# Path attention of a two-layer Perceiver block: the block inverse kept as 32x32 diagonal tiles

## The chip, the cores and the metric

The kernel runs on one core of a Trainium2 chip. The metric is the device time of one execution in microseconds (us), lower is better. The core has five engines that work at the same time: TensorE (PE, matrix multiplies; PEld is its weight load), VectorE (DVE), ScalarE (ACT), GpSimd (POOL) and SyncE (SP, which issues DMAs). They meet through semaphores. SBUF is the on-chip memory, 128 partitions wide; PSUM is where TensorE writes, 8 banks of 512 float32 values in each partition.

## The reference, cut to what matters

Input x is (16, 64, 256): 16 batch rows of 64 tokens. Six stages follow each other: cross attention, linear attention, a top-2 mixture of experts, a filtered cross attention with feed-forward, path attention, an expert-choice mixture. Only path attention changes. There are 16 heads of 16 channels, and each has two directions, so 32 systems of 64x64 for each batch row:

```python
wh = Wdir ...                       # unit vectors, (b, 32, 64, 16)
Mw  = jnp.where(strict, einsum('bhtd,bhsd->bhts', wh, wh) * bh[..., None], 0.0)
rhs = jnp.where(strict, einsum('bhtd,bhjd->bhtj', wh, kh) * bh[..., None], 0.0)
Bmat = solve_triangular(Mw + eye(t), rhs, lower=True)
# logits = q k^T - (lower part, with diagonal, of q w^T) @ Bmat
# then a causal softmax, the mean over the values, and the output projection
```

All of it is float32.

## The kernel before, in words

`path_attention` (L1688) is stage 5. It has two parts. The first (L1718 to L1943) makes the layer norm, the projections q, k, w, w times beta (`wb`) and v, and on POOL the constant masks. The second part, the batch loop (from L1996 on), is written out for the 16 batch rows without a hardware loop. Its instructions are in program order on each engine; nothing but semaphores and this order decides who works when.

The 32 systems of a batch row lie as 4 groups g by 4 heads j by 2 directions; the two directions of a pair sit in the lower and the upper 64 partitions. `mq` holds the masked transposed system and q times w, `mr` the masked right-hand side and the first inverse. The batch loop does, for batch row b:

- ACT copies the four operands of the row into one tile, `moving` (L2166). POOL spreads w and wb over pairs (`spread`, L1994) into `wt`, `wbt`, which are the weights of the products below.
- PE `strips` (L2041): two sets of 16 products with 32 rows, 128 weight columns and 128 moving columns. DVE masks them (L2251, L2254) and adds the identity (L2256); POOL makes the level masks `cT` (L2006, L2017) and the first transposed inverse (L2009, L2011), group by group.
- PE `logits` (L2067, then `small`) of the row before; DVE adds the causal mask (L2226), takes the maximum (L2232) and subtracts it (L2234); ACT takes the exponential (L2171).
- Block inverse: `inv` and `invT` are 64x64 for each system. Four levels n (block sizes 2, 4, 8, 16) of: PE `small(cT, inv)` into x, ACT copies x out (L2189), PE `small(invT, x)` and `small(x, invT)`, DVE subtracts from both inverses (L2265, L2267). In between stand the turned probabilities (L2077), the product with v (L2087) and the turned output (L2094) of the row before.
- The fifth level (block size 32) is not built into the inverse: three `small` products y = invT rhs, z = cT y, w = invT z, copied by ACT (L2206, L2209), and DVE's sol = y - w (L2274).

`small` (L2047) is the product that all of this uses. It covers one group g with 8 products of 64 rows, 64 weight columns and 64 moving columns, two at a time on the two halves of the partitions:

```python
def small(at, g, column, left, right, **flags):
    for j in range(4):
        for rows in half:
            mm = mmul(ps[rows, at, column + j * T:column + (j + 1) * T], left[rows, g, j, :],
                      right[rows, g, j, :], **flags)
    return mm
```

In float32 the trace shows two MATMUL records and two LDWEIGHTS records for each such product (transposes have one of each); counts below are of records.

Of the kernel before, what the change touches and what calls it, by code (L numbers as in the profile page):

```python
# [1687 lines left out]
def path_attention(core):  # L1688
# [10 lines left out]
    LEVELS = (2, 4, 8, 16, 32)  # L1699
    with ExitStack() as stack:  # L1700
# [6 lines left out]
        mq_mask, mr_mask = sb("upper_and_minus_incl", [P, 2, T]), sb("minus_first_and_below", [P, 2, T])  # L1707
        same, levelT = sb("same_block", [P, T]), sb("levelT", [P, len(LEVELS), T])
        firstT, causal = sb("minus_firstT", [P, T]), sb("causal", [P, T])
        ident_c = sb("ident_compact", [P, T])  # L1710
# [4 lines left out]
        with ExitStack() as inner:  # L1715
# [29 lines left out]
            def _(pool):  # L1745
# [6 lines left out]
                upper, mincl, below_first, below = mq_mask[:, 0], mq_mask[:, 1], mr_mask[:, 0], mr_mask[:, 1]  # L1752
                for o, value in ((upper, 1.0), (mincl, -1.0), (below, 1.0), (causal[:], 0.0), (below_first, 1.0),
                                 (ident_c[:], 0.0), (blocks[:], 1.0)):
                    c.link(g.memset(o, value))
                halves = (slice(0, T), slice(T, P))
                for rows in halves:
                    select(mq_mask[rows, 0], [[1, T]], -1, -1, 0.0)
                    select(mq_mask[rows, 1], [[1, T]], 0, -1, 0.0)
                    select(mr_mask[rows, 0], [[-1, T]], -1, 1, 0.0)  # L1760
                    select(mr_mask[rows, 1], [[-1, T]], -1, 1, 0.0)
                    select(causal[rows, :], [[-1, T]], 0, 1, -1e30)
                    select(ident_c[rows, :], [[-1, T]], 0, 1, 1.0, ALU.not_equal)

                def same_blocks(s, o):

                    c.link(g.memset(o[:], 1.0))
                    for rows in halves:
                        select(o[rows], [[-s, T // s], [0, s]], 0, 1, 0.0)
                        select(o[rows], [[s, T // s], [0, s]], s - 1, -1, 0.0)  # L1770

                same_blocks(2, same)
                c.link(g.tensor_tensor(firstT[:], same[:], upper, ALU.mult))
                c.link(g.tensor_scalar(firstT[:], firstT[:], -1.0, None, ALU.mult))
                c.link(g.tensor_tensor(below_first, same[:], below_first, ALU.mult))
                c.link(g.tensor_scalar(below_first, below_first, -1.0, None, ALU.mult))
                for n, s in enumerate(LEVELS):
# [4 lines left out]
                    c.link(g.tensor_tensor(m, m, upper, ALU.mult))  # L1782
# [164 lines left out]
        mq, mr = sb("mt_and_qw", [P, G, 4, 2, T]), sb("m_and_rhs", [P, G, 4, 2, T])  # L1947
        cT = sb("cT", [P, 2, G, 4, T])
        both_inv, x = sb("inv_and_invT", [P, G, 2, 4, T]), sb("x", [P, G, 4, T])
        inv, invT = both_inv[:, :, 0], both_inv[:, :, 1]  # L1950
        moving = sb("moving", [P, 2, G, 2, T])

        wt, wbt, qt = (sb(n, [P, G, 2, T]) for n in ("wt", "wbt", "qt"))
        kt = sb("kt", [P, G, T])
        vt = sb("vt", [P, 8, 2, 16])
        sol = sb("sol", [P, G, 4, T])
        y, z = sb("y", [P, G, 4, T]), sb("z", [P, G, 4, T])
        qwn = sb("qwn", [P, G, 4, T])
# [6 lines left out]
        moving_ready, spread_ready, qk_ready, vt_ready = (sem(n) for n in  # L1965
            ("moving_ready", "w_spread", "qk_ready", "vt_ready"))
        mq_ps, mq_sb, mr_ps, mr_sb, qwn_sb = (sem(n) for n in
            ("mt_qw_in_psum", "mt_qw_ready", "m_rhs_in_psum", "m_rhs_ready", "qwn_ready"))
        inv_step, start_sb, level_ready = sem("inv_step"), sem("start_ready"), sem("level_ready")
# [11 lines left out]
        with ExitStack() as inner:  # L1981
# [8 lines left out]
            def _(pool):  # L1990
# [6 lines left out]
                def batch(b, first):  # L1997
# [4 lines left out]
                    for dst, n in ((wt, 1), (wbt, 0)):  # L2002
                        spread(dst, moving[:, n, :, 0, :]).then_inc(spread_ready, 1)
# [601 lines left out]
```

## Time and profile before

| | us |
|---|---|
| median of 3 runs | 3066.19 (3065.31 to 3066.53) |
| the profiled execution | 3066.14 |
| its span, first to last instruction | 3064.4 |
| the batch loop of path attention inside it | 660, from 2160 to 2820 |
| one batch row inside the loop | 41.1 |
| busy of the whole span: PE, DVE, ACT, POOL | 2611.6, 1781.3, 1084.1, 753.5 |

The profile is of one execution. A row of it gives an engine, a line of the kernel, the operation, the tiles, the shape (for a product: rows*weight columns, then rows x moving columns) and a count; x64 is 64 records. "[idle before <-releaser]" is the time that the engine stood before the first record of the row, and what ended it; `issue` means that nothing in the profile ended it. PEclk is the share of TensorE's full clock that was granted.

### The profile page before, as it was taken

To read this page: it belongs to the slowest core of one execution; us is meant where nothing else is said; L and a number is where in the kernel's file an instruction comes from. 1 tells how busy PE (TensorE), PEld (TensorE's weight loads), DVE (VectorE), ACT (ScalarE), POOL (GpSimd) and SP (SyncE) were. 2 spreads that over 40 slices of the span, in tenths; PEclk is the share of its full clock that TensorE was granted. 3 is DMA by queue.
4 is the path that set the end of the run, shared out by engine and by line. 5 is a ranking of instruction groups with operands and counts; after the bars stand their busy time and mean duration, and the time that the engine had idled before them with its cause. 6 is when DMAs were issued, how large, how long until landed. Compare 5 with 4: busy or idle time off the path is not lost. (4 is left out here: it accounts for less than half of the span.)

```text
span 3064.4 us, 78538 instructions
## 1 busy us (share of the span) xinstructions
PE 2611.6 (85%) x34608; PEld 1894.5 (62%) x34608; DVE 1781.3 (58%) x2561; ACT 1084.1 (35%) x1702; POOL 753.5 (25%) x964
## 2 busy tenths in 40 slices
PE   5998988988897979988888878777688999888598
PEld 3565555555555545545555554443688898888487
DVE  4655545545454444569999975537666556665500
ACT  2443433434343211145555542216233333332121
POOL 6900000000000000012333323030565556663200
PEclk9999999989898779989999988889899998999699
DMA  2101001001000001132322201000000000000131
GB/s 63 33 18 34 18 18 34 18 18 32 20 2 22 0 26 36 50 94 66 93 71 82 82 17 48 0 20 14 3 4 3 4 4 4 4 3 3 55 137 41
DMA packets 24535, 99.16 MB, mean 32 GB/s; under 512 B 4824, under 2 KB 9837, under 8 KB 19502
## 3 DMA queue, kind: packets, MB, share of 16 engines
q1 hardware_dynamic: 24238, 94.57, 10.6%
q8 instruction: 264, 4.33, 0.6%
q14 instruction: 33, 0.27, 0.0%
HBM read 93.51 MB, written 1.05 MB: 31 GB/s over the span
## 5 line engine op out<-in xcount | busy, mean ns | idle before, releaser
L611 DVE TENSOR_REDUCE xa_minus_max_parts<-psum 128x4 f32<-128x1600 f32 (+1 forms) x128 | 233.9, 1827 | 221.9 <-PE psum L331 221.9
L628 DVE TENSOR_TENSOR xa_probT<-psum,xa_minus_max_spread 128x2048 f32<-128x2048 f32 (+1 forms) x112 | 239.6, 2139 | 200.5 <-PE psum L350 200.5
L315 PE MATMUL psum<-xa_ctxT,xa_wk 96*128 96x400 f32 (+1 forms) x512 | 217.7, 551 | 0.9 <-issue 0.8
L536 ACT ACTIVATE xa_probT<-xa_probT,zero_column 128x2048 f32<-128x2048 f32 (+1 forms) x112 | 209.4, 1870 | 10.8 <-DVE xa_probT L628 10.8
L2017 POOL TENSOR_TENSOR pa_cT<-pa_mt_and_qw,pa_levelT 128x256 f32<-128x256 f32 x256 | 192.6, 787 | 69.4 <-PE psum L2051 69.4
L322 PE MATMUL psum<-xa_wv,xa_ctxT 96*128 96x256 f32 (+1 forms) x832 | 208.0, 392 | 0.0
L1279 POOL TENSOR_TENSOR tk_exp_all<-tk_exp_all,tk_exp_left 128x577 f32<-128x577 f32 x64 | 120.9, 1890 | 354.2 <-ACT tk_exp_left L1400 354.2
L2189 ACT ACTIVATE pa_x<-psum 128x256 f32<-128x256 f32 x256 | 98.4, 384 | 306.3 <-PE psum L2051 294.1
L2265 DVE TENSOR_TENSOR pa_inv_and_invT<-pa_inv_and_invT,psum 128x512 f32<-128x512 f32 x192 | 132.0, 688 | 126.9 <-PE psum L2051 126.9
L716 POOL MEMSET la_v<- 128x512 f32 x1 | 0.5, 525 | 809.2 <-remote 809.2
L2051 PE MATMUL psum<-pa_inv_and_invT,pa_cT 64*64 64x64 f32 x4096 | 153.6, 237 | 40.3 <-DVE pa_prob L2226 36.7
L350 PE MATMUL psum<-xa_qb,xa_kT 32*128 32x128 f32 (+1 forms) x3328 | 132.7, 297 | 61.9 <-issue 29.4
L350 PEld LDWEIGHTS psum<-xa_qb,xa_kT 32*128 32x128 f32 (+1 forms) x3328 | 112.0, 195 | 115.4 <-issue 109.3
L322 PEld LDWEIGHTS psum<-xa_wv,xa_ctxT 96*128 96x128 f32 (+1 forms) x832 | 145.7, 185 | 60.7 <-ACT xa_v L528 27.5
L1447 DVE MAX8 tk_top<-tk_left 128x8 f32<-128x1601 f32 x96 | 175.1, 1824 | 4.1
L2051 PEld LDWEIGHTS psum<-pa_inv_and_invT,pa_cT 64*64 64x64 f32 x4096 | 144.5, 152 | 48.3 <-issue 44.4
L1449 DVE MATCH_REPLACE8 tk_left<-tk_top,tk_left 128x1601 f32<-128x1601 f32 x96 | 173.9, 1811 | 0.0
L1352 PE MATMUL psum<-tk_ctx,tk_attnT 128*128 128x192 f32 (+1 forms) x832 | 147.5, 336 | 14.7 <-ACT tk_attnT L1406 14.0
L1332 PE MATMUL psum<-tk_ctxT,tk_qwt 97*128 97x512 f32 (+1 forms) x256 | 128.2, 585 | 36.8 <-ACT tk_ctxT L1422 32.6
L2051 PE MATMUL psum<-pa_inv_and_invT,pa_x 64*64 64x64 f32 x4096 | 158.6, 220 | 0.0
L1352 PEld LDWEIGHTS psum<-tk_ctx,tk_attnT 128*128 128x128 f32 (+1 forms) x832 | 138.8, 195 | 21.3 <-ACT tk_attnT L1406 21.3
L528 ACT ACTIVATE xa_v<-psum 128x512 f32<-128x512 f32 (+1 forms) x112 | 63.5, 567 | 233.1 <-PE psum L322 233.1
(471 smaller groups left out, 5143.0 us busy)
## 6 DMA issues: line engine op xcount, KB each, us to landing
tk_ctx<-in_ctx SPq DMA_DIRECT2D x16, 1248.0 KB, 5.5
xa_ctxT<-in_ctxT SPq DMA_DIRECT2D x16, 1200.8 KB, 7.4
tk_ctxT<-in_ctxT SPq DMA_DIRECT2D x16, 1200.8 KB
ec_w<-in_ec_w SPq DMA_DIRECT2D x16, 1024.0 KB, 6.8
m_gate_up<-in_m_gate_up SPq DMA_DIRECT2D x17, 256.0 KB, 2.6
m_down<-in_m_down SPq DMA_DIRECT2D x17, 128.0 KB, 2.5
ff_w<-in_ff_w SPq DMA_DIRECT2D x2, 1024.0 KB
x_resident<-in_x SPq DMA_DIRECT2D x1, 1024.0 KB, 4.8
```

The source lines that it names most:

```text
L315: mm = mmul(ps[:, KEY_BANK[n], 0:z - a], wk[:, k, m * P:(m + 1) * P], ctxT[:, h, k, a:z], start=(k == 0), stop=(k == 1))
L322: mm = mmul(ps[0:width(c), VALUE_BANK[g], (c % 2) * D:(c % 2 + 1) * D], ctxT[:, h, k, c * P:c * P + width(c)], wv[:, k, :], start=(k == 0) ...
L350: mm = mmul(ps[0:w, j, (2 * r + c) * P:(2 * r + c + 1) * P], kT[quad[j], h, r, at:at + w], qb[quad[j], h, r, :, :].rearrange("p e t -> p ( ...
L536: a_(o, o, ACT.Exp, bias=core.zero[0:w]).then_inc(e_done, 1)
L611: v_.tensor_reduce(part[:, :, n % 2, n // 2], ps[:, 0:4, 0:z - a], AX.X, ALU.max, negate=True).then_inc(m_used, 1)
L628: v_.tensor_tensor(o[:, :, 0:chunks], got[:, :, 0:chunks], shift[0:w].unsqueeze(2).broadcast_to([w, 8, chunks, P]), ALU.add).then_inc(sub_ ...
L1352: mm = nc.tensor.matmul(flat[:, CCOL:CCOL + C], aT[0:width(c), c, :], ctx[0:width(c), h, c, :], start=(c == KC - 1), stop=(c == 7))
L1447: c.step(nc.vector.max(best, src))
L1449: c.step(nc.vector.match_replace(left[:, u % 2, :], best, src, TAKEN))
L2017: g_.tensor_tensor(cT[:, n % 2, g], mq[:, g, :, 0, :], four(levelT[:, n, :]), ALU.mult).then_inc(level_ready, 1)
L2051: mm = mmul(ps[rows, at, column + j * T:column + (j + 1) * T], left[rows, g, j, :], right[rows, g, j, :], **flags)
L2265: v.tensor_tensor(whole, whole, ps[:, 4 + g, :], ALU.subtract).then_inc(inv_sb, 1)
```

## The change

The inverse is kept only as its two 32x32 diagonal tiles for each system, so `mt`, `cT`, `inv`, `invT` and `x` have 32 columns where they had 64. `blocks32` takes the place of `small` in the four levels: one group g is 16 products of 32x32 with 32 moving columns, four at a time on the diagonal of the array. The solve is written out: the upper half of the solution (rows 0 and 2 of the four 32-row strips), a product with the corner tile of the system, a subtraction from the right-hand side, the lower half. `moving`, `kt`, `qwn`, `z` and their copies are gone; products read `wb`, `q`, `k` in place. The system of the next row is made by 96 small products (`mt_strips`) during the solve, and copied out by ACT. POOL's masks become one instruction for all four groups; the subtraction of the maximum goes from DVE to POOL; DVE makes the first inverse by 32x32 transposes. Tiles that cross a row boundary have two buffers.

The core of the diff, first PE's:

```diff
-                def small(at, g, column, left, right, **flags):
+                def blocks32(bank, column, left, right, rows=(0, 1, 2, 3), shift=0, n=Q):
                     for j in range(4):
-                        for rows in half:
-                            mm = mmul(ps[rows, at, column + j * T:column + (j + 1) * T], left[rows, g, j, :],
-                                      right[rows, g, j, :], **flags)
+                        for r in rows:
+                            mm = mmul(ps[quad[r + shift], bank, column + j * n:column + (j + 1) * n], left[quad[r], j, :],
+                                      right[quad[r], j, 0:n], start=True, stop=True)
                     return mm
+                def mt_strips(b):
+                    pe.wait_ge(wt_ready, b + 1)
+                    if b >= 2:
+                        pe.wait_ge(ot_sb, KD * (b - 1))
+                    if b:
+                        pe.wait_ge(x_sb, G * NI * b)
+                    for j in range(4):
+                        for h in range(2):
+                            for kk, column, cols in ((0, 2 * P, 0), (1, 2 * P, 1), (0, 3 * P, 1)):
+                                for g in range(G):
+                                    mm = mmul(ps[quad[2 * h + kk], g, column + j * Q:column + (j + 1) * Q],
+                                              wt[quad[g], j, h, kk * Q:(kk + 1) * Q],
+                                              wb[quad[g], j, b * T + cols * Q:b * T + (cols + 1) * Q], start=True, stop=True)
+                                    if j == 3 and h == 1 and column == 3 * P:
+                                        mm.then_inc(mt_ps, 1)
+                def qw_strips(b):
+                    pe.wait_ge(mt_sb, G * b + G)
+                    strips(0, wt, q[:, :, at(b)], qw_ps)
+                def batch(b):
+                    inv, invT = inv_of(b), invT_of(b)
+                    if b:
+                        logits_from_keys(b - 1)
+                        pe.wait_ge(sol_sb, G * b)
+                    pe.wait_ge(wbt_ready, b + 1)
+                    strips(4, wbt, k[:, :, at(b)], rhs_ps)
+                    if b:
+                        logits_from_solution(b - 1)
                     for n in range(NI):
+                        pe.wait_ge(level_ready, NI * b + n + 1)
                         for g in range(G):
...
+                            blocks32(g, 0, cT[:, n % 2, g], inv[:, g]).then_inc(x_ps, 1)
                         for g in range(G):
...
                             if n < NI - 1:
-                                small(4 + g, g, 0, invT, x, start=True, stop=True)
-                            small(4 + g, g, 4 * T, x, invT, start=True, stop=True).then_inc(t_ps, 1)
+                                blocks32(4 + g, 0, invT[:, g], x[:, g])
+                            blocks32(4 + g, P, x[:, g], invT[:, g]).then_inc(t_ps, 1)
+                        if b and n:
+                            (turn_probs, weigh, turn_out)[n - 1](b - 1)
                     for g in range(G):
+                        pe.wait_ge(inv_sb, G * (NI * b + NI - 1) + g + 1)
+                        blocks32(4 + g, 0, invT[:, g], rhs[:, g], rows=(0, 2), n=T).then_inc(y_ps_, 1)
+                    if b + 1 < B:
+                        mt_strips(b + 1)
                     for g in range(G):
+                        pe.wait_ge(y_sb, G * b + g + 1)
+                        blocks32(4 + g, 2 * P, mt[:, b % 2, g, 1], y[:, g], rows=(0, 2), shift=1).then_inc(z_ps, 1)
+                    if b + 1 < B:
+                        qw_strips(b + 1)
                     for g in range(G):
+                        pe.wait_ge(z_used, G * b + g + 1)
+                        blocks32(4 + g, 0, invT[:, g], rhs[:, g], rows=(1, 3), n=T).then_inc(sol_ps, 1)
```

POOL's, ACT's and DVE's batch, new side only:

```diff
+                def batch(b):                                   # POOL
+                    pool.wait_ge(mt_sb, G * b + G)
...
+                    level(b, 0)
+                    g_.tensor_tensor(invT_of(b), diagonal(b), over_g(firstT[:]), ALU.mult).then_inc(first_step, 1)
+                    pool.wait_ge(first_step, b + 1)
+                    g_.tensor_tensor(invT_of(b), invT_of(b), over_g(ident_c[:]), ALU.add).then_inc(firstT_ready, 1)
...
+                    level(b, 1)
+                    if b:
+                        shift(b - 1)
+                        pool.wait_ge(log_ps, G * b)
+                    spread(qt, q[:, :, at(b)]).then_inc(qt_ready, 1)
...
+                def copy_mt(b):                                 # ACT, after the four copies of y
+                    for g in range(G):
+                        act.wait_ge(mt_ps, G * b + g + 1)
+                        a.activation(mt[:, b % 2, g].rearrange("p a j c -> p (a j c)"), ps[:, g, 2 * P:4 * P], ACT.Copy
+                                     ).then_inc(mt_sb, 1)
...
+                def batch(b):                                   # DVE
                     for g in range(G):
+                        rhs_out(b, g)
+                        if b:
+                            log_out(b - 1, g)
+                    if b:
+                        maxima(b - 1)
                     for n in range(NI):
...
+                    for g in range(G):
+                        dve.wait_ge(z_ps, G * b + g + 1)
+                        v.tensor_tensor(rhs[:, g, :, 0:Q], rhs[:, g, :, 0:Q],
+                                        ps[:, 4 + g, 2 * P:3 * P].rearrange("p (j c) -> p j c", j=4),
+                                        ALU.subtract).then_inc(z_used, 1)
+                    if b + 1 < B:
+                        qw_out(b + 1)
+                        first_inverse(b + 1)
```

The mask constants on POOL are made in 32-row strips, four where there were two halves, 32 columns wide where they were 64, and for four levels where there were five.

## Rows read from the trace of the kernel before

**Rows 1.** Windows of the batch loop, a row of it, a slow stretch (us, busy and count by engine, PEclk, DMA):

```profile
2160.00:2820.00 660.00, 592.83 (x17286) 576.68 (x17286) 396.35 (x650) 220.47 (x536) 396.93 (x528) 0.94 0.01 4
2365.00:2406.00 41.00, 36.74 (x1082) 35.76 (x1082) 24.86 (x42) 13.92 (x34) 24.69 (x34) 0.96 0.02 4
2208.40:2211.80 3.40, 3.40 (x71) 3.40 (x68) 2.34 (x2) 2.31 (x6) 3.40 (x4) 0.50 0.02 5
```

**Rows 2.** Timeline of PE over one batch row (start us, us, then the group):

```profile
2407.63 1.12 PE L2067 MATMUL psum<-pa_kt,pa_qt 32*128 32x64 f32 x32 [1.76 <-DVE pa_mt_and_qw L2251]
2408.68 2.08 PE L2051 MATMUL psum<-pa_sol,pa_qwn 64*64 64x64 f32 x64
2413.46 3.48 PE L2051 MATMUL psum<-pa_inv_and_invT,pa_cT 64*64 64x64 f32 x64 [2.70 <-DVE pa_prob L2226]
...
2427.38 1.97 PE L2087 MATMUL psum<-pa_vt,pa_probT 128*128 128x32 f32 x16
...
2441.04 2.03 PE L2051 MATMUL psum<-pa_y,pa_cT 64*64 64x64 f32 x64
2442.91 2.03 PE L2051 MATMUL psum<-pa_z,pa_inv_and_invT 64*64 64x64 f32 x64
2444.87 1.17 PE L2041 MATMUL psum<-pa_moving,pa_wt 32*128 32x128 f32 x32
2445.86 1.07 PE L2041 MATMUL psum<-pa_moving,pa_wbt 32*128 32x128 f32 x32
2448.69 1.12 PE L2067 MATMUL psum<-pa_kt,pa_qt 32*128 32x64 f32 x32 [1.75 <-DVE pa_mt_and_qw L2251]
```

**Rows 3.** Timeline of PE in the first stage, products of 17 weight columns:

```profile
308.68 1.09 PE L361 MATMUL psum<-xa_probT,xa_v 128*17 128x64 f32 x64
309.70 1.61 PE L315 MATMUL psum<-xa_ctxT,xa_wk 96*128 96x400 f32 x4
```

**Rows 4.** DMA queues from 2160 to 2820 (packets, MB, share of 16 engines):

```profile
q8 instruction: 137, 2.24, 1.4%
```

**Rows 5.** DMA from 2187 to 2197, 40 slices of 0.25 us; q8 alone moved data:

```profile
GB/s 0 0 66 0 0 0 0 0 0 0 0 0 0 0 0 0 0 66 0 0 0 0 0 0 0 0 0 0 0 0 0 0 0 66 0 0 0 0 0 0
```

**Rows 6.** Timeline of the weight loads, inside that stretch and at 2733:

```profile
2193.59 0.20 PEld L2051 LDWEIGHTS psum<-pa_y,pa_cT 64*64 64x64 f32 x4
2193.99 1.77 PEld L2051 LDWEIGHTS psum<-pa_y,pa_cT 64*64 64x64 f32 x58 [0.21 <-issue]
...
2733.05 0.54 PEld L2051 LDWEIGHTS psum<-pa_z,pa_inv_and_invT 64*64 64x64 f32 x16 [0.18 <-issue]
```

**Rows 7.** DMA from 2729 to 2735, 40 slices of 0.15 us:

```profile
GB/s 0 0 0 0 0 0 0 109 0 0 0 0 0 0 0 0 0 0 0 0 0 0 0 0 0 0 0 0 0 0 0 0 0 0 109 0 0 0 0 0
```

**Rows 8.** Timeline of PE after a hardware loop jumped back; DMA from 293.5, slices of 0.125 us:

```profile
296.58 2.09 PE L350 MATMUL psum<-xa_qb,xa_kT 32*128 32x128 f32 x32 [6.07 <-issue]
...
GB/s 0 0 234 0 0 0 0 0 0 0 0 0 0 0 0 0 0 0 0 0 0 0 0 0 0 0 0 0 0 131 0 0 0 0 0 0 0 0 0 0
q8 instruction: 2, 0.03, 3.0%
```

**Rows 9.** Groups of POOL, DVE and ACT (line, shapes, count | busy us, mean ns | idle):

```profile
L1140 POOL TENSOR_TENSOR powers_t<-powers_wr,filter_zr 128x512 f32<-128x512 f32 x2 | 2.5, 1267 | 0.2
L2341 POOL TENSOR_TENSOR ec_hot<-ec_hot,ec_p 128x1024 f32<-128x1024 f32 x8 | 19.8, 2513 | 39.2 <-PE psum L2369 39.2
L2265 DVE TENSOR_TENSOR pa_inv_and_invT<-pa_inv_and_invT,psum 128x512 f32<-128x512 f32 x192 | 132.0, 688 | 126.9 <-PE psum L2051 126.9
L2267 DVE TENSOR_TENSOR pa_inv_and_invT<-pa_inv_and_invT,psum 128x256 f32<-128x256 f32 x64 | 27.0, 422 | 36.4 <-PE psum L2051 34.3
L2234 DVE TENSOR_TENSOR pa_prob<-pa_prob,pa_mx 128x1024 f32<-128x1024 f32 x16 | 19.6, 1226 | 0.5
L2189 ACT ACTIVATE pa_x<-psum 128x256 f32<-128x256 f32 x256 | 98.4, 384 | 306.3 <-PE psum L2051 294.1
L2181 ACT ACTIVATE pa_q<-psum 128x128 f32<-128x128 f32 x32 | 7.1, 275 | 60.6 <-PE psum L2094 60.6
```

More of the change, by code:

```diff
@@ L1751, in _ @@
                 c.step(g.memset(eps[:], 1e-6))
[L1752 to L1761, printed above, removed]
+                for o, value in ((upper, 1.0), (mincl, -1.0), (below, 1.0), (causal, 0.0), (ident_c, 0.0), (blocks, 1.0)):
+                    c.link(g.memset(o[:], value))
@@ L1762, in _ @@
+                for rows in (slice(0, T), slice(T, P)):
+                    select(mincl[rows, :], [[1, T]], 0, -1, 0.0)
+                    select(below[rows, :], [[-1, T]], -1, 1, 0.0)
                     select(causal[rows, :], [[-1, T]], 0, 1, -1e30)
-                    select(ident_c[rows, :], [[-1, T]], 0, 1, 1.0, ALU.not_equal)
+                quads = [slice(Q * n, Q * n + Q) for n in range(4)]
+                for rows in quads:
+                    select(upper[rows, :], [[1, Q]], -1, -1, 0.0)
+                    select(ident_c[rows, :], [[-1, Q]], 0, 1, 1.0, ALU.not_equal)
@@ L1781, in _ @@
                     c.link(g.tensor_tensor(same[:], m, same[:], ALU.add))
-                    c.link(g.tensor_tensor(m, m, upper, ALU.mult))
+                    c.link(g.tensor_tensor(m, m, upper[:], ALU.mult))
                 select(blocks[:], [[-16, P // 16], [0, 16]], 0, 1, 0.0)
@@ L2035, in _, with strips @@
                 mmul = nc.tensor.matmul
-                def strips(at, left, right, done):
+                def strips(first_bank, left, right, done, **flags):
                     for j in range(4):
                         for g in range(G):
-                            mm = mmul(ps[:, at + g, j * P:(j + 1) * P],
-                                      left[quad[g], j, :, :].rearrange("p a t -> p (a t)"),
-                                      moving[quad[g], right, j, :, :].rearrange("p a t -> p (a t)"), start=True, stop=True)
-                            if j == 3:
+                            mm = mmul(ps[:, first_bank + g, j * T:(j + 1) * T],
+                                      left[quad[g], j, :, :].rearrange("p a t -> p (a t)"), right[quad[g], j, :],
+                                      start=flags.get("start", True), stop=flags.get("stop", True),
+                                      skip_group_check=not flags.get("stop", True))
+                            if j == 3 and done is not None:
@@ L2123, in batch @@
-                            small(g, g, 0, cT[:, n % 2], inv, start=True, stop=True).then_inc(x_ps, 1)
+                                pe.wait_ge(first_ready, b + 1)
+                                pe.wait_ge(*((log_sb, G * (b - 1) + g + 1) if b else (qw_sb, g + 1)))
+                            else:
+                                pe.wait_ge(inv_sb, G * (NI * b + n - 1) + g + 1)
+                            if b and g == 2 and n == 2:
+                                pe.wait_ge(pt_sb, 2 * b)
@@ L2141, in batch @@
+                    if b + 1 < B:
+                        qw_strips(b + 1)
                     for g in range(G):
-                        ready((z_sb, G * b + g + 1))
-                        small(4 + g, g, 0, invT, z, start=True, stop=True).then_inc(w_ps, 1)
+                        pe.wait_ge(z_used, G * b + g + 1)
+                        blocks32(4 + g, 0, invT[:, g], rhs[:, g], rows=(1, 3), n=T).then_inc(sol_ps, 1)
+                mt_strips(0)
+                qw_strips(0)
                 for b in range(B):
-                    batch(b, b == 0)
@@ L2147, in _ @@
-                logits(B - 1, last=True)
+                    batch(b)
+                logits_from_keys(B - 1, last=True)
+                logits_from_solution(B - 1)
                 turn_probs(B - 1)
```

278 lines of the change are left out of this document (123 added, 155 removed).

## The prediction

> **What bounds the kernel now.** I read the windows first: the batch loop takes 660 us of the span, and in one row of 41 us PE is busy 36.7, DVE 24.9, POOL 24.7 and ACT 13.9 [rows 1]. So PE sets the pace there. The timeline of PE shows how: a row begins every 41.06 us (2407.63 to 2448.69), and PE stands only twice, 1.76 us until DVE has masked the system and 2.70 us until DVE has masked the logits [rows 2]. Everything else is PE issuing products. After the second stand it works for 3.4 us at a granted clock of 0.50, its lower level (1.2 GHz) [rows 1], and 64 records take 3.30 us there instead of 1.87.
>
> How fast does PE issue? In the solve 64 records start in 1.87 us (2441.04 to 2442.91), 29.2 ns each [rows 2]. Each has a weight load beside it (17286 and 17286 in the loop [rows 1]), so an instruction leaves every 14.6 ns. The reader is to see a second limit close behind this one. The DMA queue q8 carries PE's instructions: 137 packets of 16 KB for 34572 records, 252 per packet [rows 4, 1], in 1.4% of 16 engines over 660 us, 1.1 us a packet. Where PE runs at full speed the packets start 3.75 and 4.0 us apart [rows 5], which is the 3.7 us that 252 records last. And PE runs dry: at 2193.99 and 2733.05 weight loads stand with nothing in the profile to release them [rows 6]. The packet before the first began in the slice at 2191.25 to 2191.5, the one before the second at 2730.05 to 2730.2 [rows 5, 7]: the stand ends 2.6 and 2.9 us after the packet's start, its length of 1.1 and some 1.5 us more, both times, and the next packet starts 1.1 to 1.4 us later, 4.05 us after the one before in [rows 7]. So one block is fetched ahead, not many. The jump of a hardware loop shows the same: packets 3.4 us apart (27 slices of 0.125), PE's first product (296.58) 2.8 us after the first packet and 0.55 before the second [rows 8]. The loop lives just under its instruction supply.
>
> **The change part by part.**
>
> Instructions of PE, one batch row, in MATMUL records. Before: 1082 [rows 1]. After, from the diff (records are twice the products, once for transposes): levels, four times 128 for x, three times 256 and once 128 for the update, 1408, where they were 704; y, z and the lower solve 64 each, as the three products before; system of the next row 192; q w and right-hand side 32 each, where two sets of 32 were; logits 32 and 64; the turned and weighed parts 26 as before. Sum 1978, 83% more, and as many weight loads: 3956 instructions, or 15.7 blocks of 252 where there were 8.6.
>
> Array time of these. A 32x32 product was not run before. From the nearest rows: halving the moving columns and going from two to four at once makes 29.2 into 7.3 ns a record; the products of 17 weight columns and 64 moving columns, four at once, start every 15.9 ns (64 in 1.02 us [rows 3]), and they are of the size that is twice as long. From above, a record could cost what it costs now, 29.2. I take 7.3 for the array. Levels and system: 1600 x 7.3 = 11.7 us; z, two at once, 64 x 14.6 = 0.9; y, lower solve and logits 3 x 1.87; the two strip sets 2 x 0.99; keys 1.05; weighing 16 x 119 ns = 1.9; ten transposes at the same 119, 1.2 [rows 2]. That is 24.4 us, so the array would no longer be the bound.
>
> Supply. 15.7 blocks a row at the interval of a starved fetch. The rows give 3.4 (jump), 3.75 and 4.0 us [rows 5, 8]. When PE empties a block faster, the request for the next should come earlier in it, so I take the shortest, 3.4; 4.0 is the upper end. Whole loop: 16 x 3956 = 63296 instructions, 251 blocks, 251 x 3.4 = 853 us. Nearly each block is shorter than that for the array: the one with the 16 weighings is 1.9 + 0.8 us, half a block of y with half of the system 1.9 + 0.5. So the array hides behind the supply, not the other way round.
>
> Clock. In the levels PE would then stand more than half of the time. In the rows its clock fell to half after stands that long [rows 1, 2]. For the 32x32 products this costs nothing, since they still fit under 3.4 us. For y, the lower solve, logits, strips and weighing it doubles 11.7 us, of which the supply hides part. Between 0 and 10 us a row; I take 2, since the slow stretch of [rows 1] was over after 3.4 us in which PE worked: 32 us.
>
> Waits. The stands of 1.76 and 2.70 us go as such (the system is made in the row before; logits and right-hand side are masked in turns). New ones: `qw_strips` waits for ACT's four copies of `mt`; 256 wide they take 0.38 each [rows 9], 1.6 us with the latency, against z's 128 instructions. Behind the copy stands POOL: level mask, first inverse and identity, 3 x 1.27 for 512 columns [rows 9], 3.8 us; then DVE's four transposes (128 wide, not in the trace; ACT's 0.28 to DVE's 0.42, 1.2 us), and behind them in DVE's order the eight maskings, 3.2. That is 8.2 us from the copy to the last mask, while PE has the 448 instructions of q w, lower solve, keys, right-hand side and logits, 6.0 us of supply, and the first three groups of level 0, 1.3. Left: 0.9 us. I count 0.8 a row, 13 us; bounds 0 and 3 us, what the two stands cost now.
>
> The subtraction of the maximum on POOL costs 2.5 instead of 1.23 us [rows 9]. Between it and the turned probabilities PE has two levels, six blocks, so it is hidden in rows 1 to 15 and adds 1.3 us after the last. ACT's x copies halve (0.38 to 0.28) and DVE's updates shrink from 0.69 to 0.42 [rows 9]; both wait for PE. The four copies of `moving`, POOL's copy of k and ACT's of q w run beside PE today and bring nothing now. The mask constants: some 16 more short selects on POOL, beside the projections; if that cover failed, under 5 us. Tile buffers change no time.
>
> Sum. Loop: 853 + 32 + 13 = 898 us, plus 1 at the end, against 660: +239. On the profiled execution (3066.14, practically the median of 3066.19): 3305 us. A batch row would take 56 us.
>
> The Trainium skill speaks against this. "Runtime: NRT & Kernel Launch", section "Instruction fetch mechanics", says that instructions come in 16 KiB blocks, that PE holds eight, and that crossing a boundary is mostly hidden since a dispatch floor of about 20 cycles per instruction is slower. The stands at 2193.99 and 2733.05 show that it is not hidden at 14.6 ns an instruction, and 14.6 ns held for hundreds is under 20 cycles of the 1.2 GHz sequencer (16.7 ns, an estimate from that page and "TensorE: Matmul & The Clock Gate"). With that floor instead of the supply a row would be 66 us.
>
> **The rivals.**
>
> A, the supply keeps up (a deeper prefetch once blocks are emptied fast). Then the array and the waits count: 24.4 us a row, plus 0.7 for the `mt` copy, 1.6 for the masks before level 0 and about 1.3 around probabilities and output, 28 us; 660 - 16 x 13.1 + 1 = 451, and 2857 us. For it: 64 products with their loads left in 1.02 us [rows 3], 8 ns an instruction. Against it: 128 instructions are half a block, and the fastest stretch of the loop, the solve, gives 3.7 us to 252 [rows 2]. The skill's page on the runtime, with fetches hidden, is this rival without its dispatch floor. This is the other side. It turns on the block interval: under 2.6 us (41.1 / 15.7) the kernel gets faster.
>
> B, blocks overlap in part, so that the 1.5 us after a packet is not paid each time: 1.1 + 1.1 = 2.2 us, 34.5 a row, with waits and heavy blocks 37: -66, 3001 us. For it: the packets are short. Against it: both stands and the jump came with 1.5 us or more.
>
> C, a record costs the same whatever its size: 29.2 ns. Levels, system and z 1664 x 29.2 = 48.6, the rest 11.7, a row of 60.3: +307, 3373 us. Against it the 15.9 ns of [rows 3]. "TensorE: Matmul & The Clock Gate" of the Trainium skill, "Back-to-back issue gap", gives a floor of about 25 ns between matmuls however small. By it a row is an estimated 53.3 us and the kernel near 3262; the 15.9 ns disagrees.
>
> D, the change doesn't cut the array time because the diagonal tiles don't run at once: 1600 records at 14.6 ns, 23.4 + 12.7 = 36 us, under the supply, so the time is mine.
>
> **How the numbers follow.** Forecast with D 0.78, C 0.05, A 0.10, B 0.07. Bounds of the forecast: blocks at 3.25 with no clock loss and no wait, 816 us, +157: 3223; blocks at 4.0 with 2 us of clock and 0.8 of waits, 1004 + 46, +390: 3456. The range is 3160 to 3450: it leaves out A, B and a twentieth of the forecast. Two runs of this kernel are told apart from 0.2% (6 us). Slower: D, C and nearly no other, 0.82; faster A and most of B, 0.16; same 0.02, where B's interval comes to 2.6 us.
>
> **What would show it.** Right: some 250 packets on q8 in the loop at 3.3 to 3.6 us without a gap; PE's share of busy in the levels well under one half, stands before PE and its weight loads ended by `issue`; a row of 52 to 60 us; the granted clock in the loop clearly under 0.94; no engine over 60% busy. Wrong: packets closer than 2.6 us; rows of 128 level records that start in about 1 us one behind the other (A), or in 3.7 us evenly (C); stands in the levels that end at DVE or ACT.

## The result

The changed kernel takes 3414.7 us (median of 4 runs, 3407.6 to 3417.9) where the kernel before takes 3065.8 (4 runs, 3060.9 to 3066.5): a ratio of 1.114, with an interval of 1.112 to 1.115. It is 349 us slower; the prediction said 3305 us, 239 slower, with a range up to 3450. The profiled execution has a span of 3410.5 us, 346 more than before, and its batch rows account for that: counted from the first key product of one row to that of the next, the mean of ten rows is 62.96 us instead of 41.28, and 16 x 21.7 is 347. The number lies in the range but 110 us over the forecast, so what speaks for the mechanism is not the number: rival C, at 3373 us, came nearer to it. The traces and the runs below decide.

### The profile page after: what moved, and what is told of

It is laid out like the page before. It is cut to its first block and busy times, and to the rows that moved or that the text cites. A ratio compares the mean times of both kernels' runs of the same rounds, so it can differ in the third digit from the quotient of the medians.

```text
span 3410.5 us, 106580 instructions
## 1 busy us (share of the span) xinstructions
PE 2740.5 (80%) x48944; PEld 1996.3 (59%) x48944; DVE 1633.9 (48%) x2545; ACT 1035.7 (30%) x1686; POOL 562.8 (17%) x623
## 5 line engine op out<-in xcount | busy, mean ns | idle before, releaser
L2302 DVE TENSOR_TENSOR pa_inv_and_invT<-pa_inv_and_invT,psum 128x256 f32<-128x256 f32 x192 | 80.9, 421 | 381.7 <-PE psum L2065 380.4
L2065 PE MATMUL psum<-pa_x,pa_inv_and_invT 32*32 32x32 f32 x6144 | 135.5, 222 | 150.1 <-issue 150.1
L2228 ACT ACTIVATE pa_x<-psum 128x128 f32<-128x128 f32 x256 | 70.9, 277 | 486.2 <-PE psum L2065 466.9
L2065 PE MATMUL psum<-pa_inv_and_invT,pa_x 32*32 32x32 f32 x8192 | 160.1, 227 | 56.2 <-issue 56.2
L2065 PEld LDWEIGHTS psum<-pa_x,pa_inv_and_invT 32*32 32x32 f32 x6144 | 108.9, 135 | 163.8 <-issue 163.7
L2065 PEld LDWEIGHTS psum<-pa_inv_and_invT,pa_x 32*32 32x32 f32 x8192 | 137.1, 141 | 54.9 <-issue 54.9
L2065 PE MATMUL psum<-pa_inv_and_invT,pa_cT 32*32 32x32 f32 x8192 | 123.1, 227 | 36.7 <-issue 36.5
L2065 PEld LDWEIGHTS psum<-pa_inv_and_invT,pa_cT 32*32 32x32 f32 x8192 | 112.3, 141 | 47.7 <-issue 44.6
```

Of the source, the lines that this page charges most:

```text
L2065: mm = mmul(ps[quad[r + shift], bank, column + j * n:column + (j + 1) * n], left[quad[r], j, :], right[quad[r], j, 0:n], start=True, stop= ...
```

## The profile after

The page's lines first: busy time of PE, the granted clock in 40 slices of the span, and the queue that carries PE's instructions.

```profile
PE 2740.5 (80%) x48944; PEld 1996.3 (59%) x48944; DVE 1633.9 (48%) x2545; ACT 1035.7 (30%) x1686; POOL 562.8 (17%) x623
...
PEclk9999999899986998999997889555556565565699
...
q8 instruction: 375, 6.14, 0.8%
```

The windows answer to [rows 1]: the same 660 us of the loop, one row, and the part of it with q w, lower solve, keys, right-hand side and logits.

```profile
2160.00:2820.00 660.00, 468.36 (x20751) 439.94 (x20755) 163.62 (x419) 113.81 (x342) 140.23 (x119) 0.57 0.02 4
2410.50:2474.60 64.10, 44.40 (x1980) 41.58 (x1979) 15.71 (x40) 10.96 (x33) 12.98 (x11) 0.61 0.02 4
2405.00:2417.70 12.70, 12.70 (x228) 12.17 (x224) 5.15 (x17) 1.53 (x4) 2.80 (x3) 0.50 0.01 3
```

A row has 1980 records (1978 were counted). DVE, ACT and POOL are busy for 15.7, 11.0 and 13.0 us of its 64.1, where the row before had 24.9, 13.9 and 24.7 of 41. PE is idle for 20 us of the row, and over the loop its clock is at 0.57 instead of 0.94. The waits of PE say who owns the 20 us; this is the view of waits over fifteen rows, from 2220 to 3160 (line that waited, what ended the wait, us in total, times, longest), all of its lines:

```profile
PE psum L2065 <- issue: 237.5, 133, 2.7
PE psum L2080 <- issue: 20.0, 15, 2.5
PE psum L2125 <- issue: 1.7, 2, 1.3
PE psum L2115 <- issue: 1.4, 1, 1.4
PE psum L2054 <- issue: 0.7, 1, 0.7
```

Not one of them ends at DVE, ACT or POOL. The two stands of before, at DVE [rows 2], are gone as the change meant; PE now waits for its own instructions. The timeline of PE over a row answers to [rows 2]:

```profile
2403.20 1.91 PE L2065 MATMUL psum<-pa_y,pa_mt_and_corner 32*32 32x32 f32 x62 [1.64 <-issue]
2405.04 1.98 PE L2054 MATMUL psum<-pa_q,pa_wt 32*128 32x64 f32 x32
2406.95 3.62 PE L2065 MATMUL psum<-pa_rhs,pa_inv_and_invT 32*32 32x64 f32 x64
2410.51 1.98 PE L2098 MATMUL psum<-pa_k,pa_qt 32*128 32x64 f32 x32
2412.27 1.93 PE L2054 MATMUL psum<-pa_k,pa_wbt 32*128 32x64 f32 x32
2414.13 3.68 PE L2107 MATMUL psum<-pa_sol,pa_minus_qw 64*64 64x64 f32 x64
2417.74 1.42 PE L2065 MATMUL psum<-pa_inv_and_invT,pa_cT 32*32 32x32 f32 x128
...
2422.46 0.21 PE L2065 MATMUL psum<-pa_x,pa_inv_and_invT 32*32 32x32 f32 x1 [2.40 <-issue]
...
2426.14 0.26 PE L2065 MATMUL psum<-pa_x,pa_inv_and_invT 32*32 32x32 f32 x2 [2.32 <-issue]
...
2430.12 0.69 PE L2065 MATMUL psum<-pa_inv_and_invT,pa_cT 32*32 32x32 f32 x35 [2.06 <-issue]
```

The 128 records of the first level start in 1.27 us (2417.74 to 2419.01), 9.9 ns each: the small products do run beside each other. Then comes the pattern of the levels: a little over a microsecond of work, then a stand of 1.6 to 2.5, every 3.5 to 4.0 us. Over the first two levels PE is busy for half of the time:

```profile
2417.70:2438.00 20.30, 10.15 (x770) 9.44 (x768) 4.65 (x10) 3.25 (x9) 7.39 (x6) 0.67 0.02 4
```

The queue has the same beat. From 2419 to 2427, in slices of 0.2 us, it moved two packets (compare [rows 5, 7]):

```profile
GB/s 0 0 0 82 0 0 0 0 0 0 0 0 0 0 0 0 0 0 0 0 0 0 0 82 0 0 0 0 0 0 0 0 0 0 0 0 0 0 0 0
```

By their records these packets begin at 2419.66 and 2423.70 and last 1.34 and 1.02 us. The stands end at 2422.46 and 2426.14, which is 1.46 and 1.42 us after a packet's end, the 1.5 us of the kernel before. Of 115 distances between packets from 2230 to 2700 the shortest is 3.26 us, the median 3.78 and the mean 4.05; 85% are under 4.5, with a mean of 3.74. Over all 230 distances from 2220 to 3160 the median is 3.76, and that is the value used below. Of the 17 distances over 4.5, the longest (up to 7.6) touch the part from q w to the logits, where a window above shows a clock of 0.50 and 12.7 us; six, of 4.5 to 5.1, stand by the weighing, or by the turned output and y, at a clock of 0.50 to 0.55.

## The experiments

Kernels sent together were timed beside the kernel before on the same chip (3060.7 to 3066.5 us). The row is the mean of ten, from one profile; packets are those of q8.

| kernel | PE records a row | packets a row | us | row, us | clock in the loop |
|---|---|---|---|---|---|
| before | 1082 | 8.6 | 3065.8 | 41.3 | 0.94 |
| after | 1978 | 15.5 | 3414.7 | 63.0 | 0.58 |
| dose | 2234 | 17.6 | 3527.6 | 70.5 | 0.57 |
| cols | 1978 | 15.5 | 3407.4 | 62.4 | 0.82 |
| fill | 2010 | 15.8 | 3444.4 | 65.3 | 0.61 |
| warm | 2014 | 15.8 | 3428.6 | 63.1 | 0.90 |
| mt48 | 1882 | 14.8 | 3398.6 | 62.1 | 0.58 |
| half | 1178 | 9.3 | 3024.0 | 38.8 | 0.54 |
| wide64 | 1114 | 8.7 | 3046.4 | 39.7 | 0.92 |
| wide64b | 1114 | 8.7 | 3010.0 | 37.3 | 0.97 |
| before_dose | 1338 | 10.6 | 3135.0 | 44.9 | 0.96 |
| wide64h | 666 | 5.3 | 2855.4 | 27.6 | 0.76 |

**More instructions, hardly more work: dose.**

```diff
+                            if n in (1, 2):
+                                blocks32(g, 0, cT[:, n % 2, g], inv[:, g])
                             blocks32(g, 0, cT[:, n % 2, g], inv[:, g]).then_inc(x_ps, 1)
```

> The changed kernel with the 128 records of x at the second and third level issued twice (the same values into the same place): +256 records, +512 instructions a row, 2 blocks. Supply theory: +2 x 3.75 = 7.5 us a row, +120 us: 3535 (3510 to 3550), fetches on q8 up by 32. Rival, latency between the engines (ACT's copies, DVE's updates) fills the levels: the records cost 9.9 ns each where they have to be issued, 2.5 us a row or less, +40: 3455 or below.

3527.6 us, +113. Two more packets a row (2.1) and 7.5 us more: 3.6 us each. At the 9.9 ns a record of the changed kernel the array time of the 256 added records is an estimated 2.5 us, a third of that.

**More work, the same instructions: cols.**

```diff
-                            blocks32(g, 0, cT[:, n % 2, g], inv[:, g]).then_inc(x_ps, 1)
+                            pair = both_inv[:, b % 2, g].rearrange("p a j c -> p (a j) c")
+                            blocks32_wide(g, 0, cT[:, n % 2, g], pair, 0).then_inc(x_ps, 1)
```

(`blocks32_wide` moves 64 columns; the two updates are changed in the same way.)

> The changed kernel with every product of the four levels moving 64 columns instead of 32 (the neighbouring tile's columns with it, which nobody reads): the same 3956 instructions a row and the same values, but the array work of 1408 records a row doubled, +10.3 us at the full clock, +20.6 at half. Supply theory: 2816 instructions are 11 blocks of 3.5 us, 38.5 us, and the doubled products need 20.6 us at the full clock, 41 at half: between -8 us a row (the fuller array raises the granted clock and the other parts of the row run at full speed) and +4: 3290 to 3480. If the array set the pace: +10 to +20 us a row, 3575 to 3740. What the clock does under it is the second question: it stays at 0.58 if small products are not the reason for it.

3407.4 us, and 1.114 times the kernel before beside it, the ratio of the changed kernel. Doubling the array work of 1408 records a row cost nothing. Its timeline shows the fuller work: 28 records take 0.75 us (2426.31 to 2427.06), where the changed kernel has 29 in 0.38 (2430.63 to 2431.01), both at about half clock.

```profile
2422.07 1.45 PE L2076 MATMUL psum<-pa_inv_and_invT,pa_cT 32*32 32x64 f32 x89
2425.77 0.69 PE L2076 MATMUL psum<-pa_inv_and_invT,pa_cT 32*32 32x64 f32 x34 [2.25 <-issue]
2426.31 0.94 PE L2076 MATMUL psum<-pa_x,pa_inv_and_invT 32*32 32x64 f32 x28
2427.06 1.04 PE L2076 MATMUL psum<-pa_inv_and_invT,pa_x 32*32 32x64 f32 x28
```

The part from q w to the logits is at half clock as in the changed kernel, in its windows:

```profile
2463.10:2475.90 12.80, 12.80 (x229) 12.22 (x232) 5.19 (x16) 1.54 (x4) 3.46 (x3) 0.50 0.01 3
```

The clock over the loop rose from 0.58 to 0.82 and brought under 1 us a row, since it rose in the levels (1.00 from 2422 to 2424 in cols), where PE waits for the queue.

**Work put into the stands: fill.**

```diff
+                            mmul(ps[:, 4 + g, 3 * P:4 * P], core.ident[:], core.ident[:], start=True, stop=True)
                             if n < NI - 1:
```

> The changed kernel with 16 products a row added in the levels, one ahead of each group's update (identity by identity, 128 columns, into a part of PSUM that nobody reads): 64 instructions, a quarter of a block, but 3.4 us of array work at the full clock, 6.8 at half. Supply theory with the clock as its second part: the stands are long enough to hold this work, so +0.9 us a row (+15 us) for the instructions; and if the granted clock rises because PE stands less, the parts of the row that run at half clock now (upper and lower solve, right-hand side, logits) get shorter, up to -8 us a row: 3300 to 3430. Rival, the array is the bound in the levels: +3.4 to 6.8 us a row, 3470 to 3525.

3444.4 us, +30, between the two ranges and in neither: twice what the instructions alone should cost, and under the rival's price of 3.4 us a row and more. Stretches without a start (over 0.5 us) fell from 19.8 to 10.5 us a row, so most of the new work lay in them. Why the row still grew by 2.3 us is not shown. The clock hardly followed (0.61): less standing alone did not bring it back.

**What the clock costs: warm.** It is cols with 18 wide products more:

```diff
+                            if (j, h) != (3, 1):
+                                for g in (2 * h, 2 * h + 1):
+                                    mmul(ps[:, g, 0:P], core.ident[:], core.ident[:], start=True, stop=True)
...
+                        mmul(ps[:, 4 + g, 3 * P:4 * P], core.ident[:], core.ident[:], start=True, stop=True)
```

> cols (every level product moving 64 columns) with 18 products of 128x128 by 128 columns a row added where PE still stands at the supply ahead of the heavy parts: 14 between the strips of the next row's system and 4 ahead of the corner products, into parts of PSUM that nobody reads. 72 instructions, 0.28 of a block, +1.0 us a row. In cols the granted clock was at full speed in the levels, fell in the starved stretch of system and corner, and then q w, lower solve, keys, right-hand side and logits took 12.7 us at half clock (2463.16 to 2475.85) where the same 224 records take 6.9 us in wide64 at full clock. If the clock is what those parts pay, and the filled stretch keeps it up: 12.7 becomes 7 to 8, the row loses 3.5 to 5 us, 3330 to 3355. If they pay their supply or a wait: +1 us a row, 3415 to 3430. If the clock falls all the same, the run says nothing on its price.

3428.6 us (ratio 1.120 to before, 1.114 to 1.126). The median misses the forecast and lies in the range of the rival, that these parts pay their supply or a wait. Its rows tell more. In 11 of 15 rows the clock was up from the keys to the logits, which took 3.8 us instead of 7.0; one such stretch, from q w on, in the windows:

```profile
2356.90:2363.90 7.00, 7.00 (x237) 6.67 (x229) 4.23 (x14) 1.54 (x4) 3.35 (x3) 1.00 0.02 5
```

So 5.7 of the 12.7 us were the clock. But seven such rows whose strips ran at full clock too last 59.4 to 62.8 us, 61.4 in the mean; less the 1.0 us that the added instructions are estimated to cost, that is only 1.9 under the 62.4 of cols, on which warm is built, and 2.5 under the changed kernel's 63.0. Inside warm it is less still: the four rows in which these parts took 6.6 to 7.0 us, strips at full clock, last 62.2 in the mean, 0.7 more than the seven, for some 3 us of longer work inside the row. The rest is given back. While the slow stretch runs, the queue gets ahead: the packets there stand 7.1 us apart (2408.34 and 2415.41), and in the 4.25 us behind them the changed kernel started 476 instructions, nearly two blocks. At full clock that lead is missing; that the lead is the whole of what is given back is argued, not shown. Three rows took 69.2 to 71.0 us: in the one at 2405 the clock fell in the strips, where the added products are at half clock (four records in 1.22 us) and the strips take about 11 us instead of 7. They carry the mean up.

**Fewer products for the next row's system: mt48.**

```diff
...
+                            moving = wb[quad[g], j, b * T + Q:b * T + T].unsqueeze(1).broadcast_to([Q, 2, Q])
+                            mmul(ps[:, g, 2 * P:4 * P].rearrange("p (s j c) -> p s j c", s=2, j=4)[:, :, j, :],
+                                 wt[quad[g], j, :, :].rearrange("p a t -> p (a t)"), moving, start=True, stop=True)
...
```

> The changed kernel with the system of the next row made by 48 products instead of 96 (one of 128 weight columns for columns 32 to 63 written to both slots, then two of 32 for the first 32): 96 records or 192 instructions fewer a row, same values. Supply theory: 0.75 of a block, -2.8 us a row, -45 us: 3370 (3350 to 3385). Rival, the array sets the pace at its lower clock: 96 records at 14.6 ns are 1.4 us, the products that replace them are wider, so -0 to -15 us: 3400 to 3415.

3398.6 us, -16: at the edge of the rival's range (3400 to 3415), not the supply's -45. In the row shown the stand ahead of the corner went (1.64 us), but the wide products are at half clock, 0.63 us for each 8:

```profile
2402.99 0.70 PE L2079 MATMUL psum<-pa_wb,pa_wt 32*128 32x64 f32 x8
2403.62 0.36 PE L2083 MATMUL psum<-pa_wb,pa_wt 32*32 32x32 f32 x16
```

The strips take 3.5 us in all, where the 192 small records took 2.2 and the stand 1.6. Both limits lie close together in this stretch, so fewer instructions bring little there.

**Two fifths fewer instructions: half.**

```diff
-        mt, qw = sb("mt_and_corner", [P, 2, G, 2, 4, Q]), sb("minus_qw", [P, 2, G, 4, T])
+        mt, qw = sh("mt_and_corner", [P, 2, G, 2, 4, Q]), sb("minus_qw", [P, 2, G, 4, T])
```

(`sh` makes a bfloat16 tile; `rhs`, `cT`, `both_inv`, `x` and `y` are changed in the same way.)

> The changed kernel with mt, cT, inverse, x, y and the right-hand side stored in bfloat16, so that a product of two of them is one record instead of two: levels 704 records instead of 1408, the three solve steps 96 instead of 192, 1178 a row instead of 1978; the same products, waits and order. It computes in lower precision. Supply theory: 1600 instructions fewer, 6.25 blocks of 3.5 us, -22 us a row: 41 us, 3065 us (3030 to 3130). Rival, latency between the engines or the clock makes the row: it loses the array time alone, 5 to 10 us a row: 3250 to 3340.

3024.0 us, -391, 6 us below the forecast's range, with the 32x32 tiles, the order and the semaphores as they are in the changed kernel, and with a clock of 0.54. The row lost 24.1 us for 6.2 packets, 3.9 each. ACT's x copies and DVE's updates take as long as in the changed kernel (276 and 416 ns, 277 and 421 there), so the row did not shrink by them; that the halved array work did it does not fit cols, where doubling it cost nothing. This run separates supply from clock best: the clock is lower than in any other, and the kernel is faster than the one before. With the row at 38.8 us some waits that the changed kernel hides come out, about 2 us a row; from the view of PE's waits, 2230 to 2790:

```profile
PE psum L2066 <- issue: 92.2, 53, 2.8
PE psum L2081 <- issue: 30.1, 22, 2.5
PE psum L2055 <- ACT pa_mt_and_corner L2206: 8.5, 10, 0.9
PE psum L2099 <- DVE pa_minus_qw L2258: 8.2, 14, 0.6
```

**The change without its small tiles: wide64, wide64b.**

```diff
...
-                            blocks32(g, 0, cT[:, n % 2, g], inv[:, g]).then_inc(x_ps, 1)
+                            blocks64(g, 0, cT[:, n % 2, g], inv[:, g]).then_inc(x_ps, 1)
...
```

(Tiles, masks and the other products of the levels are 64 wide too, and the next row's system takes 32 records where it took 192.)

> The changed kernel in every respect (no moving copies, the next row's strips during the solve, corner product, shift on POOL), except that inverse, level blocks and x are kept 64 wide and multiplied as 64x64 products: 704 records in the levels instead of 1408, 32 for the system of the next row instead of 192, 1114 a row instead of 1978. Supply theory (256 instructions of PE cost about 3.75 us, whatever is in them): 2228 instructions are 8.8 blocks, 33 us, array time about the same, with waits 36 to 38 us a row instead of 64.1: 3415 - 16 x 27 = 2980 us (2950 to 3040), under the kernel before too. Rival (the new order is what costs: POOL behind the copy of mt, the masks before level 0, the split upper and lower solve): the row stays over 41 us and the kernel over 3065.

3046.4 us: ratio 0.993 (0.992 to 0.995). Right in sign, but 66 us over the forecast and 6 over its range. The timeline shows a stand of 2.39 us and a half-clock level behind it; DVE's transposes waited there for POOL's third operation (such a stand, of up to 2.7 us, is in seven of some fourteen rows):

```profile
2411.25 3.49 PE L2073 MATMUL psum<-pa_inv_and_invT,pa_cT 64*64 64x64 f32 x64 [2.39 <-DVE pa_prob L2277]
...
2406.66 2.35 POOL L2017 TENSOR_TENSOR pa_inv_and_invT<-pa_inv_and_invT,pa_ident_compact 128x1024 f32<-128x1024 f32 x1
...
2409.05 1.42 DVE L2268 STREAM_TRANSPOSE pa_inv_and_invT<-pa_inv_and_invT 128x256 f32<-128x256 f32 x4 [4.60 <-POOL pa_inv_and_invT L2017]
```

> wide64 with POOL making the first inverse (two operations) ahead of the first level's mask instead of behind it. In wide64 PE stands 2.39 us before the first level, for DVE, whose transposes began when POOL's third operation of 2.36 us ended, and works at half clock for 64 records behind the stand. The transposes can start 2.36 us earlier; the mask is then last on POOL, at the time at which the identity was. If that chain is what holds PE: -2 to -3.5 us a row, 3046 - 32 to 56: 2990 to 3015. Rival, the logits' maskings on DVE are last anyway: 3035 to 3046.

```diff
-                    level(b, 0)
                     g_.tensor_tensor(invT_of(b), diagonal(b), over_g(firstT[:]), ALU.mult).then_inc(first_step, 1)
                     pool.wait_ge(first_step, b + 1)
                     g_.tensor_tensor(invT_of(b), invT_of(b), over_g(ident_c[:]), ALU.add).then_inc(firstT_ready, 1)
+                    level(b, 0)
```

3010.0 us, ratio 0.984 (0.982 to 0.987): it beats both kernels in full precision. The stand is 0.20 us:

```profile
2433.29 2.54 PE L2073 MATMUL psum<-pa_inv_and_invT,pa_cT 64*64 64x64 f32 x64 [0.20 <-POOL pa_cT L1992]
```

**The dose in the kernel before: before_dose.**

```diff
+                            if n in (1, 2):
+                                for j in range(4):
+                                    for rows in quad:
+                                        mmul(ps[rows, g, 2 * P + j * 32:2 * P + (j + 1) * 32], cT[rows, n % 2, g, j, 0:32],
+                                             cT[rows, n % 2, g, j, 0:32], start=True, stop=True)
```

> The kernel before with 128 products of 32x32 added a row, at the second and third level ahead of x, into a part of PSUM that nobody reads: 256 records, 512 instructions, 2 blocks, the dose that made the changed kernel 113 us slower. If the kernel before lives just under its supply: +2 x 3.5 us a row, +112 us, 3178 (3150 to 3200). If its supply has slack, the added records cost their array time, 7.3 to 9.9 ns each, 2 to 2.5 us a row: +30 to +40, 3100.

3135.0 us, +74 over the runs of before beside it (ratio 1.026, 1.022 to 1.029), between the two. Two packets more a row cost 3.6 us. The kernel before has slack, but only a few microseconds a row: its packets are 4.8 us apart in the mean.

**Both together: wide64h**, wide64b with the tiles in bfloat16, the `sh` of half.

> wide64b with mt, cT, inverse, x, y and the right-hand side in bfloat16 (lower precision): levels 352 records instead of 704, solve steps 96 instead of 192, about 666 a row, 1332 instructions, 5.2 blocks. Supply theory: 5.2 x 3.6 = 19 us, no longer the bound; the latency between PE, ACT and DVE in the levels (ACT's copies and DVE's updates of 0.69 us, four a level) and the clock should then make the row, 25 to 30 us: 2810 to 2890. Rival: a product's record costs the same in bfloat16 and the row is bound elsewhere: above 2950.

2855.4 us, ratio 0.932 (0.929 to 0.936), as expected. PE's short stands in the levels now end at DVE and ACT:

```profile
2418.30 0.31 PE L2074 MATMUL psum<-pa_inv_and_invT,pa_cT 64*64 64x64 bf16 x8 [0.36 <-DVE pa_inv_and_invT L2309]
2418.81 0.31 PE L2074 MATMUL psum<-pa_inv_and_invT,pa_cT 64*64 64x64 bf16 x8 [0.19 <-DVE pa_inv_and_invT L2309]
```

At 5.3 packets a row the supply is no longer the limit. Whether the lower precision may be had is not a question of time.

**The subtraction back on DVE: shift_dve.**

```diff
+                    dve.wait_ge(max_done, b + 1)
+                    v.tensor_tensor(prob[:], prob[:], mx[:].unsqueeze(2).broadcast_to([P, 16, T]), ALU.subtract
+                                    ).then_inc(shifted, 1)
```

(Both calls of `shift` on POOL are taken out.)

> The changed kernel with the subtraction of the maximum back on DVE, behind the maximum itself. The prediction counted its move to POOL as hidden in rows 1 to 15 and 1.3 us at the very end. Supply theory: nothing in the row, -1 us at the end: 3405 to 3420, no difference that can be told. Rival, the move delays the exponentials and with them the turned probabilities that PE waits for: -1 us a row or more, below 3400.

3415.3 us against 3414.7: no difference.

## Why the prediction was right, and where its sizes were off

The mechanism held: PE starves at its instruction supply, at 1.8 times the instructions, and in the levels and the next row's system, 1600 of the 1978 records, the array hides behind it. dose (instructions added, array hardly), cols (array doubled, no instruction added) and half (instructions taken away, same tiles) show it from three sides. 349 us were measured where 239 were forecast, inside the range. By its steps, per row, 56.2 forecast and 63.0 measured:

- **Records and packets.** 1978 forecast and 1980 read; 15.7 blocks forecast, 15.5 packets read, so a block holds 256 instructions, not 252.
- **Block interval, 3.4 us. This is the term that was mis-sized.** The median over the loop is 3.76, and the distances under 4.5 us have a mean of 3.74 in the changed kernel, 3.71 in cols, 3.80 in warm, 3.75 in dose. 15.5 x 3.76 is 58.3 us against the 53.4 of the forecast: 4.9 us a row, 78 of the 110 us that are missing. I took the jump's two packets [rows 8], the shortest of the distances, and argued that a block emptied faster is asked for sooner. It isn't by much: in the levels a packet begins 1.0 to 1.4 us after the stand ends, as it did before, though PE has started nearly all of the block's 128 records by then. With the 3.75 of [rows 5] the same sum gives 3393 us.
- **Clock, 2 us.** 63.0 less 58.3 leaves 4.7 us a row in the long intervals. warm gets 1.9 back against cols, 2.5 against the changed kernel, where the clock stays up, so the size was near by that run; whether the other 2.2 to 2.8 us are the clock's no run shows. I argued that the slow stretch would be over after 3.4 us as in [rows 1]; it lasted 12.7. Ahead of it in each row lies the starved stretch of strips and corner, and in warm, which fills that stretch, the clock was up in 11 of 15 rows.
- **Waits, 0.8 us.** None: the chain from the copy of `mt` to the masks was in time, since the half-clock stretch gave it 12.7 us and not the 7.3 that I counted. In half, whose row is shorter, PE does wait: 0.85 us for the copy of `mt` in ten of some fourteen rows, and 0.6 in each for the masks of q w, which is near what I counted. In wide64, with operations twice as long and the clock up, the same chain did cost up to 2.39 us.
- **Array, 24.4 us.** Not a bound in the levels. 9.9 ns a record for 128 in a row, where 7.3 were taken, and 13 at half clock (29 in 0.38 us): 128 records, a block with their loads, are then 1.7 us, still under the block interval, as the prediction said. From q w to the logits PE is busy for all of the 12.7 us.
- **Hidden edits.** In the groups of POOL, ACT and DVE, which answer to [rows 9],

```profile
L2007 POOL TENSOR_TENSOR pa_prob<-pa_prob,pa_mx 128x1024 f32<-128x1024 f32 x16 | 30.4, 1900 | 183.2 <-DVE pa_mx L2276 183.2
L2228 ACT ACTIVATE pa_x<-psum 128x128 f32<-128x128 f32 x256 | 70.9, 277 | 486.2 <-PE psum L2065 466.9
L2302 DVE TENSOR_TENSOR pa_inv_and_invT<-pa_inv_and_invT,psum 128x256 f32<-128x256 f32 x192 | 80.9, 421 | 381.7 <-PE psum L2065 380.4
```

  the subtraction on POOL, 1.9 us and not 2.5, costs nothing (shift_dve). ACT's x copies take 277 ns and DVE's updates 421, as forecast, and both stand idle for PE: that shortening them brought nothing is read from this, no run tests it.
- **Rivals.** A and B needed packets under 2.6 us apart; the closest two are 3.26. C is refuted by the 9.9 ns. D is refuted too: tiles one behind the other would take 14.6.
- **What would show it.** 3.3 to 3.6 us between packets, a row of 52 to 60 us and no engine over 60% busy were too low: 3.76, 63.0, and PE at 71% of the loop, because records at half clock count as busy for longer. PE's share in the levels, well under one half by the prediction, is one half (10.15 of 20.30 us). And a sign that was listed for rival A does come, once a row: the 128 records of the first level start in 1.27 us, out of the lead that the queue got in the half-clock stretch. The stands behind them decide against A.

The rule weighed in the prediction, of the Trainium skill's "Runtime: NRT & Kernel Launch", section "Instruction fetch mechanics" (fetch mostly hidden behind a dispatch floor of about 20 cycles), doesn't hold for this stream. The row of 63.0 us is near the 66 that this floor would give, but only by its length: 128 records and as many loads started in 1.27 us, 5.0 ns an instruction, and 15.5 fetches a row are in the open.

What stays open is what sets the 1.4 us between a packet's end and PE's next start, and why a packet lasts 0.9 us at one time and 1.3 at another. Nothing here changes either.

## What to carry to other kernels

Count the instructions of a change, not only its array time: at an instruction every 14.6 ns, as in the kernel before, the supply was nearly as close a limit as the array. Here it gave 256 instructions in some 3.7 us, and where PE would get through them faster than that a smaller tile bought nothing, because it took more instructions for the same work. Look for stands that end at `issue` and for the beat of the instruction queue in the kernel as it is, and take the interval from its busiest stretch (3.75 and 4.0 us here), not from a single jump (3.4). Separate a change that has several parts: here the order (next row's strips in the solve, no moving copies) was worth 0.7%, 1.6% with one operation of POOL moved, and the small tiles, in the levels and in the next row's system, cost 368 us on top of it.

## What was not expected of the hardware

- A stretch at half clock is partly free when the supply is the limit: the queue gets about one block ahead in it. 5.7 us of longer work cost some 2 (1.9 against cols, 2.5 against the changed kernel).
- The granted clock does not follow PE's busy share in the profile. From 2240 to 2740 fill, its level products moving 32 columns, had PE busy for 426.3 of 500 us at a clock of 0.61, and cols, whose level products move 64, for 370.7 at 0.82. Part of this is the other way round: at half clock the same records count as busy for longer.
- Doubling the array work of the levels (cols) left the ratio to the kernel before as it was, 1.114.
- Storing operands in bfloat16 was worth 391 us: a product of two of them is one record instead of two, 1178 a row instead of 1978, and the operations of ACT and DVE became no shorter.
